# Unread matmuls on the identity tile at three stage starts and around the first maxima, and doubled maxima pieces, in a two-layer transformer kernel

## What is computed

```
x = x + L0_attn(layernorm(x))   # linear attention, 32 heads of 128, decays, silu, gate, out
x = x + L0_ffn(layernorm(x))    # silu(h1) * h3, 512 -> 1376 -> 512, with LoRA terms
x = x + L1_attn(layernorm(x))   # q, k, v clipped to 8; layer norm of q and k; 32 heads of 16
x = x + L1_ffn(layernorm(x))    # gelu, 512 -> 2048 -> 512
# L1_attn: rows 0..1023 are one sequence here
scores = where(causal, q @ k.T * 16 ** -0.5 + slope * (k_pos - q_pos), -inf)
attn   = softmax(scores) @ v
```

## Time and profile before

| | us |
|---|---|
| median of 3 runs | 2048.5 |
| lowest and highest | 2048.13, 2048.84 |
| the profiled execution | 2049.02 |
| its span, first to last instruction | 2047.1 |
| PE busy in the span | 1921.2 (94%) |
| VectorE (DVE) busy | 856.7 (42%) |
| GpSimd (POOL) busy | 676.0 (33%) |
| ScalarE (ACT) busy | 436.7 (21%) |
| mean granted PE clock | 0.959 |

### The profile page before, as it was taken

One profiled execution on the slowest core, in us unless ns is written; L12 is line 12 of the kernel. 1 busy time (PEld: TensorE's weight loads), 2 busy tenths in 40 slices (PEclk: granted clock), 3 DMA queues, 4 the chain that ended last, 5 costly groups with the idle time before them and its releaser, 6 DMA issues. The chain is left out here.

```text
span 2047.1 us, 26945 instructions
## 1 busy us (share of the span) xinstructions
PE 1921.2 (94%) x10439; PEld 1508.9 (74%) x10439; DVE 856.7 (42%) x1586; ACT 436.7 (21%) x534; POOL 676.0 (33%) x816
## 2 busy tenths in 40 slices
PE   6999999999999999999999689998967999978998
PEld 4888888888888888888888578886733444356877
DVE  5242442432433424324324533305565888532332
ACT  3111111111121111111111020002303666631111
POOL 4322231311313222313100165436701221238765
PEclk9999999999999999999999889998966999988999
DMA  4010110110110101101100123102071333012333
GB/s 156 29 57 29 57 35 22 56 56 28 34 51 28 56 28 56 42 15 56 36 8 13 52 68 87 54 1 83 1 99 22 53 59 56 2 47 67 97 88 97
DMA packets 41124, 101.47 MB, mean 50 GB/s; under 512 B 7712, under 2 KB 12448, under 8 KB 36576
## 3 DMA queue, kind: packets, MB, share of 16 engines
q1 hardware_dynamic: 39784, 97.95, 16.5%
q10 hardware_dynamic: 1272, 2.61, 0.9%
HBM read 84.28 MB, written 2.10 MB: 42 GB/s over the span
## 5 line engine op out<-in xcount | busy, mean ns | idle before, releaser
L146 PE MATMUL a_ps<-a_xh_h,a_w_h 128*128 128x512 f32 x768 | 307.1, 400 | 3.4 <-POOL a_w_l L270 2.0
L148 PE MATMUL a_ps<-a_xh_h,a_w_l 128*128 128x512 f32 x768 | 301.1, 392 | 0.0
L147 PE MATMUL a_ps<-a_xh_l,a_w_h 128*128 128x512 f32 x768 | 300.3, 391 | 0.0
L60 POOL TENSOR_TENSOR tick<-neg_half 128x1 f32<-128x1 f32 x108 | 36.5, 338 | 659.9 <-PE a_ps L148 615.6
L390 DVE TENSOR_TENSOR x<-x,a_ps 128x1024 f32<-128x1024 f32 x64 | 78.2, 1222 | 260.0 <-PE a_ps L148 260.0
L1234 ACT ACTIVATE a1h_pr<-a1h_ps 128x1024 f32<-128x1024 f32 (+1 forms) x192 | 153.3, 812 | 92.4 <-PE a1h_ps L1364 71.2
L146 PEld LDWEIGHTS a_ps<-a_xh_h,a_w_h 128*128 128x128 f32 x768 | 144.8, 189 | 31.6 <-DVE a_xh_l L101 4.0
L148 PEld LDWEIGHTS a_ps<-a_xh_h,a_w_l 128*128 128x128 f32 x768 | 144.3, 188 | 30.3
L147 PEld LDWEIGHTS a_ps<-a_xh_l,a_w_h 128*128 128x128 f32 x768 | 144.8, 189 | 27.9
L1384 PE MATMUL a1h_ps<-a1h_KT,a1h_QT 64*128 64x512 f32 (+2 forms) x384 | 141.7, 466 | 24.9 <-DMA a1h_QT<-a_qslope 13.9
L1384 PEld LDWEIGHTS a1h_ps<-a1h_KT,a1h_QT 64*128 64x128 f32 x384 | 70.2, 205 | 98.8 <-DVE a1h_mx L1283 34.9
(11 more groups left out here) (189 smaller groups left out, 3819.5 us busy)
## 6 DMA issues: line engine op xcount, KB each, us to landing
a_raw<-in_a_wqkgv SPq DMA_DIRECT2D x30, 1024.0 KB
f_raw<-in_f_w SPq DMA_DIRECT2D x64, 256.0 KB, 2.6
f_raw<-in_f_w SPq DMA_DIRECT2D x33, 320.0 KB, 2.9
a_raw<-in_a_wout SPq DMA_DIRECT2D x32, 256.0 KB, 5.2
a_cst<-in_a_cst SPq DMA_DIRECT2D x32, 129.0 KB
a1h_KT<-a_k_h SPq DMA_DIRECT2D x64, 64.0 KB
a1q_raw<-in_a_wqkv SPq DMA_DIRECT2D x3, 1024.0 KB
a1h_QT<-a_q_h SPq DMA_DIRECT2D x40, 64.0 KB
```

Of the source, the lines that this page charges most:

```text
L60: nc.gpsimd.tensor_tensor(top["tick"][:, :], top["neg_half"][:, 0:1], top["neg_half"][:, 1:2], ALU.mult)
L146: nc.tensor.matmul(out, w_hi, x_hi, start=start, stop=False)
L147: nc.tensor.matmul(out, w_hi, x_lo, start=False, stop=False)
L148: return nc.tensor.matmul(out, w_lo, x_hi, start=False, stop=stop)
```

## The change

A helper `warm` issues a number of matmuls of the identity tile with itself (128x128 by 128x128, float32) into a place in PSUM that nothing reads before it is written again. FFN0, the QKV stage and FFN1 begin with 24 of them, and have 6 more after each of their first tiles' transposes (4, 3 and 4 tiles). The heads stage begins with 50, has 8 ahead of each of the first two rows, and 24 ahead of the first score. Each of the first 56 maxima pieces is issued twice into the same bank, and only the second signals VectorE. Nothing else moves, no wait is added, and no other engine's instructions change. Lines after the helper move by six and more: mm3 is L152 to L154 then.

```diff
@@ -139,6 +139,12 @@
             last = nc.tensor.transpose(b["ps"][:, t, k * P:(k + 1) * P], b["xn"][:, t % 2, k * P:(k + 1) * P],
                                        b["ident"][:, :])
         last.then_inc(s("ln_transposed"), 1)
+
+
+def warm(nc, top, out, times):
+
+    for _ in range(times):
+        nc.tensor.matmul(out, top["ident"][:, :], top["ident"][:, :], start=True, stop=True)
 
 
 def mm3(nc, out, w_hi, w_lo, x_hi, x_lo, start, stop):
@@ -785,7 +791,10 @@
                 nc.tensor.matmul(DELTA, a2_st[0:LR, :], b2_st[:, :], start=True, stop=True
                                  ).then_inc(s("delta_done"), 1)
 
-            ln_tensor(nc, pe, s, b, range(4))
+            warm(nc, top, ps[:, 7, 0:P], 24)
+            for t in range(4):
+                ln_tensor(nc, pe, s, b, (t,))
+                warm(nc, top, ps[:, 7, 0:P], 6)
             lowered(0)
             ln_tensor(nc, pe, s, b, range(4, 6))
             hidden(1, 0, 0)
@@ -1016,7 +1025,10 @@
                                                top["ident"][:, :])
                 last.then_inc(s("turned"), 1)
 
-            ln_tensor(nc, pe, s, b, range(FIRST))
+            warm(nc, top, ps[:, 7, 0:P], 24)
+            for t in range(FIRST):
+                ln_tensor(nc, pe, s, b, (t,))
+                warm(nc, top, ps[:, 7, 0:P], 6)
             for k in range(KT):
                 if k == KT - 1:
                     ln_tensor(nc, pe, s, b, (FIRST,))
@@ -1372,7 +1384,7 @@
                                                 start=False, stop=True)
                 last.then_inc(s("score_made"), 1)
 
-            def piece(p, k):
+            def piece(p, k, repeat=1):
 
                 at = MAX_AT[(p, k)]
                 if k == 0:
@@ -1381,9 +1393,10 @@
                 h, t, c, width, _ = PIECES[k]
                 rows = slice(ROWS * h, ROWS * (h + 1))
                 w = max(width, 2 * P)
-                nc.tensor.matmul(out[:, 0:w], QT[p % SETS][rows, t * P:(t + 1) * P],
-                                 KTs[p % SETS][rows, c * BANK:c * BANK + w], start=True, stop=True
-                                 ).then_inc(s("max_made"), 1)
+                for _ in range(repeat):
+                    last = nc.tensor.matmul(out[:, 0:w], QT[p % SETS][rows, t * P:(t + 1) * P],
+                                            KTs[p % SETS][rows, c * BANK:c * BANK + w], start=True, stop=True)
+                last.then_inc(s("max_made"), 1)
 
             def max_row(p):
 
@@ -1447,18 +1460,22 @@
                     yield max_row(q)
                 yield from pieces(q + 1, 2, AHEAD)
 
+            warm(nc, top, S[1][:, 1, 0:P], 50)
             for k in range(NP):
-                piece(0, k)
-            piece(1, 0)
-            piece(1, 1)
+                piece(0, k, 2)
+            piece(1, 0, 2)
+            piece(1, 1, 2)
+            warm(nc, top, S[1][:, 1, 0:P], 8)
             max_row(0)
             for k in range(2, NP):
-                piece(1, k)
-            piece(2, 0)
-            piece(2, 1)
+                piece(1, k, 2)
+            piece(2, 0, 2)
+            piece(2, 1, 2)
+            warm(nc, top, S[1][:, 1, 0:P], 8)
             max_row(1)
             for k in range(2, AHEAD):
-                piece(2, k)
+                piece(2, k, 2)
+            warm(nc, top, S[1][:, 1, 0:P], 24)
             for g in range(QUADS):
                 made, strand = 0, maxima(g)
                 for u, upto in enumerate(paced(g)):
```

## The result

The changed kernel takes **2060.1 us** (median of 4 runs, 2059.76 to 2067.49) against 2048.3 of the kernel before beside it: 1.0068 times, with an interval of 1.0044 to 1.0091. The forecast was 2061.6, slower by 13.1; measured 11.8. The profiled execution is the one of 2067.49, with a span of 2065.6 us and a mean clock of 0.972 (0.959 before): PE is at 2.4 GHz for more of a longer time. In the experiments, three single executions of 3159, 4747 and 5966 us lie far outside all others and are left out of the ratios.

A forecast was written before the change was run, and what follows sets the result against it. PE bounds the kernel, a matmul chain mostly at 2.4 GHz; only idle PE or 1.2 GHz stretches yield time. Heads +10.0, FFN0 +2.2, QKV 0, FFN1 +0.9 make +13.1 us: 2061.6 us against the 2048.5 median, range 2046.5 to 2069.0.

The forecast's parts named there:

- the likeliest case: Heads stage: clock rises in the 50 products, drops in the maxima; 2061.6 us, chance 0.58.
- Price of a product: All packs: an identity product costs PE 0.22 us at full clock and 0.43 us at half.
- FFN0, +2.2: FFN0's start: 24 products and the sixes make the first mm3 3.7 us late, 1.5 comes back: +2.2 us.
- QKV stage, 0: QKV stage's start: PE 1 to 2 us late, covered by a later 2.09 us wait for a clip: 0.
- FFN1, +0.9: FFN1's start: first mm3 some 3.2 us late, 2.3 comes back at full clock: +0.9 us (0 to 3).
- The clock falls in the maxima: Heads stage: after the 50 products, 64-row pieces lose the clock a few us in and do not regain it.
- Rival 1: Heads stage: only pauses count, so the clock holds through the maxima; +0.8 us, 2049.3, no change; chance 0.27.
- Rival 2: Clock holds in the heads and packs hide in PE's waits; faster, 2044.7 us; chance 0.10.
- rival 3: All packs: identity products do not count as work or raise the clock late; about 2085 us; chance 0.05.
- PE-bound pieces for 32.9 us: Maxima: 13% of the doubled pieces run at DVE's pace in 4 us, the other 87% at half clock take 32.9.
- The first score was to be 16.8 late: Heads stage: PE ready for the first score at 1563.6 instead of 1546.76, 16.8 us late.
- Quad 0, a gain of 6.8: Quad 0, entered at full clock and dense, takes 35.8 us instead of 42.6: 6.8 us gained (0 to 11.6).

The follow-up runs named there:

- experiment 1: The changed kernel run again, unchanged, against the kernel before: 2060.0 us, 1.0055 times.
- experiment 7: experiment 3 with the first matmul of each doubled maxima piece over 128 rows instead of 64: 2082.7 us, 1.0162 times the kernel before.
- experiment 8: experiment 4 plus one identity product ahead of each of the first 16 scores of quad 0: 2050.6 us, 1.0008 times the kernel before.
- experiment 2: Kernel before plus only the identity products at the three layer norms, heads stage as before: 2053.9 us, 1.0018 times.
- experiment 3: Kernel before plus only the heads part (50, 8, 8 and 24 products, doubled pieces), norms as before: 2059.4 us, 1.005 times.
- experiment 6: Kernel before plus only the doubled maxima pieces, no identity product anywhere: 2051.8 us, 1.0004 times.
- experiment 4: Kernel before plus only 34 identity products behind the last maxima piece, ahead of the first score; single pieces: 2049.8 us, 1.0008 times.
- experiment 12: experiment 4 plus one identity product ahead of each of the first 4 scores of quad 0: 2048.9 us, 0.9987 times the kernel before.
- experiment 9: experiment 4 with its 34 products on 64 rows of the identity tile instead of 128: 2054.3 us, 1.0026 times the kernel before.
- experiment 5: experiment 3 with single instead of doubled maxima pieces: 2056.4 us, 1.0022 times the kernel before.
- experiment 10: experiment 3 without the two packs of eight products: 2052.3 us, 1.0014 times the kernel before.

## Why the prediction was right

**The direction and the size.** +11.8 measured (+10.1 in experiment 1), +13.1 forecast, by the likeliest case. The course was the forecast one: the maxima start late, the clock falls in them, the old wait is used up and the first score is late. Its terms did not all hold, and that the number came so near is in part luck, as the last paragraph says.

**Price of a product.** 0.22 us at full clock and 0.43 at half, right in every pack. What the price left out: beside 64-row matmuls a product costs 0.39 to 0.42 at full clock (experiments 7 and 8). In the change this touches few places.

**FFN0, +2.2.** Measured +2.9 and +2.3, and +2.3 in experiment 2. The first mm3 was to be 3.7 us late: 4.4 in the profile after, 3.7 in experiment 2.

**QKV stage, 0.** The wait of the earlier trace rows is still 2.09 us long. From the stage's start to the heads' first piece it is +0.4 in experiment 2. Up to the first product, against the 1499.5 from which the forecast counted, it is +0.5 in experiment 1 and +2.2 in the profile after, and -1.7 in experiment 3, which has no pack there: 0 within the scatter.

**FFN1, +0.9.** Measured -0.8 and -0.9, though the first mm3 came 3.0 us late (forecast 3.2): more is given back than the 2.3 that I counted. But without any pack there this stretch was 213.4 us long in experiment 6 and 210.4 in experiments 4 and 12, so 213.9 is no gain either. The term is 0 within the scatter.

**The clock falls in the maxima.** This was the point on which the case hung, and it fell 5.5 us after the first piece in the profile after, 4.2 in experiment 1, 8.5 in experiment 3. That 64-row matmuls do not win it back is now shown, for the pieces by experiment 6 and with the same count and columns by experiment 9. That their rows are also why it fell is argued: the run that was to test it, experiment 7, changed the pace too. Rival 1, by which only pauses count and the clock holds, is out: it did not hold, and in experiment 7 it fell after a stretch in which the profile shows no pause. By the Trainium skill (TensorE: Matmul & The Clock Gate, section "Why this matters for your kernels"), drops in the middle of a kernel are avoided by leaving no idle gaps between bursts of matmuls; that row of experiment 7 disagrees with it. Rival 2 needed a clock that holds too, and rival 3 is out by experiment 4, where the products raised the clock after 4.6 us.

**PE-bound pieces for 32.9 us: mis-sized.** The term that was off is "PE-bound now and not raising it" for 87% of the pieces. The eights did win the clock back, after each of the two rows, for 6.8 us and 8.3 us in the profile after; I had left this to the edge of the range. So from first product to first score the heads took 58.9 and 59.4 us, where the sum had 64.1. In the profile after the pieces with their rows took 32.0, not 37.9, and the last pack 5.6, not 7.2; the 50 products took 14.3, not 13.0, and the eights 7.1, not 6.0. Where the clock does stay down, experiment 6, they take the forecast's 37 us. The first score was to be 16.8 late; measured within its stretch it was 13.8 and 12.7.

**Who pays for the lateness.** The sum put it on three places: the 50, the doubling and the eights. The runs weigh two of them against the 9.5 us of experiment 3: leaving out the eights takes off 7, with intervals that don't overlap, and leaving out the doubling 3 by the medians and 6 by the ratios, with intervals that do. The doubling alone costs nothing that shows (experiment 6), since the old wait covers it. No run has the 50 alone. From the QKV stage's start to the heads' first piece it is 11.5 us more than before in the profile after, 8.6 in experiment 1 and 7.3 in experiment 3, so the 50 use up most of the 11.04 us of wait, and what comes on top is paid; that they would be free by themselves follows from this for the last two figures, but is not shown.

**Quad 0, a gain of 6.8.** Right in size, 35.0 us against the forecast's 35.8, but only where the clock holds. I took it as certain that quad 0, entered at full clock, keeps it. In the profile after it entered at 1.00 and lost it 5.2 us later (-1.4 instead of -6.8), in experiments 4, 5 and 12 likewise, in experiments 1, 3, 7 and 10 not. What the change costs from FFN0 on is 14.7 us in the profile that lost it (the 18.5 of the table less the 3.8 ahead of every change) and 6.2 in the one that kept it. The medians, +11.8 and +10.1, lie between, and which of their runs kept the clock is not on record. The forecast's 13.1 comes of a first score that is 3 to 4 us too late and a quad 0 that always keeps the clock. In an execution that loses it, the second error is 5.4 us the other way and the two nearly cancel; in one that keeps it, the forecast is some 7 us too high. That the medians came so near is luck.

## What to carry to other kernels

Raising PE's clock ahead of a stretch pays only if the stretch keeps it. Count what the stretch itself does to the clock, in matmuls of how many rows, before paying for the raise: here a late pack hidden in a wait cost nothing and gave nothing that the medians show, and with eight more full-row products in the thin start it was 3.6 us ahead, likely but not shown. Put filler where PE already waits, and behind, not ahead of, the work that DVE needs first: 14.3 us of products at the head of a chain used up most of a wait that would have covered what was added behind them.

## What the runs showed of the hardware

- Half-height matmuls keep PE busy and do not raise the clock: 14.00 of 14.00 us at 0.50 with 64 rows, a rise from 1.2 to 2.4 GHz after 4.6 us with 128 (experiments 9 and 4). The products of 128 rows, which raised it, are nearly all zeros, and the pieces, on real data, did not raise it (experiment 6), so it wasn't zeros that kept it down.
- The clock fell after a stretch in which the profile shows PE busy for 5.70 of 5.70 us (experiment 7), and stayed at 0.50 for 27.30 busy us with every other matmul of full height.
- Alternating 128-row and 64-row matmuls of 512 columns start 0.42 us apart at full clock, full-row ones alone 0.23, and 0.72 against 0.43 at half, while two 64-row ones on different halves of the rows take 0.50 us together. Nothing in the instruction count shows it.
- The same program gets or loses the clock in quad 0 from one execution to the next: 35.0 and 41.2 us. Times of the kernel before spread over 15 us (2039.4 to 2054.8 on one chip), and the shortest of them has the highest mean clock (0.964 against 0.958 of the longest); where in the kernel it differs is not on record. So a profile is a sample here, and medians of ten runs compare to 2 to 4 us.
